# Joining the programs of attention, FFN and recurrence, and leaving out the unread matmuls

## What is computed

```
x = layernorm(x + attention(x))          # 16 heads of 16, widened to 32 latents, rotary, causal softmax
x = layernorm(x + fp4_ffn(x))            # blocks of 16 rounded to the FP4 grid before each linear layer
x = layernorm(x + recurrence(x))         # t = rmsnorm(x); 512 steps in time:
                                         #   state = tanh(state @ tanh(a) + t_step @ b)
                                         #   out   = state @ c + skip * t_step
                                         # then x + out @ w_out.T + b_out
x = layernorm(x + channel_mix(x))        # r * (relu(k)^2 @ W_v.T), each from a mix with the token before
```

## Time and profile before

| | |
|---|---|
| median of the runs shown (2317.63 and 2320.34) | 2318.99 us |
| the profiled execution: time / span | 2320.48 / 2318.7 us |
| its mean granted TensorE clock | 0.979 |
| PE busy | 2209.4 us, 95% |
| DVE busy | 1706.9 us, 74% |
| ACT busy | 1060.6 us, 46% |
| POOL busy | 1187.8 us, 51% |
| instruction packets of PE (queue q8) | 108, 1.77 MB |

### The profile page before, as it was taken

The page is one execution under the profiler, slowest core; times in us unless marked ns, Lnnn a source line. Parts: engine busy times, 40 slices in busy tenths (PEclk is TensorE's granted clock), DMA queues, the critical chain, the costliest instruction groups (busy, mean ns, idle before and its releaser), DMA issues. The chain is left out here.

```text
span 2318.7 us, 90879 instructions
## 1 busy us (share of the span) xinstructions
PE 2209.4 (95%) x36556; PEld 1542.3 (67%) x36556; DVE 1706.9 (74%) x4854; ACT 1060.6 (46%) x2707; POOL 1187.8 (51%) x1674
## 2 busy tenths in 40 slices
PE   6999999999999999959999999997999999997997
PEld 3556665556655555536777777776888888885775
DVE  3788888888887777749999999982555555454997
ACT  2656565655666665532222222231444444442444
POOL 3555555655555555525666666662444444441333
PEclk8999999999999999989999999997999999998999
DMA  2211111111111111120100000100101011011232
GB/s 92 91 56 64 57 65 65 65 63 58 57 64 65 65 61 60 52 69 22 33 32 32 32 32 32 34 20 29 32 32 36 32 34 33 32 32 46 84 95 77
DMA packets 101627, 117.73 MB, mean 51 GB/s; under 512 B 10672, under 2 KB 80080, under 8 KB 101456
## 3 DMA queue, kind: packets, MB, share of 16 engines
q1 hardware_dynamic: 101456, 115.44, 15.1%
HBM read 48.29 MB, written 33.55 MB: 35 GB/s over the span
## 5 line engine op out<-in xcount | busy, mean ns | idle before, releaser
L1474 ACT ACTIVATE r_state<-ps_state 128x64 f32<-128x64 f32 x1024 | 228.6, 223 | 295.8 <-PE ps_state L1573 290.7
L1570 PE MATMUL ps_state<-r_state,later_pairs_a 64*64 64x32 f32 x8192 | 334.4, 219 | 19.4 <-ACT r_state L1474 12.5
L1570 PEld LDWEIGHTS ps_state<-r_state,later_pairs_a 64*64 64x64 f32 x8192 | 295.2, 135 | 79.2 <-issue 60.7
L1573 PE MATMUL ps_state<-r_state,later_pairs_a 64*64 64x32 f32 x8192 | 334.6, 220 | 2.8 <-issue 2.8
L423 DVE CUSTOM_DVE_ANT_0 ps_near<-ps_near,mask 128x512 f32<-128x512 f32 (+1 forms) x512 | 270.5, 589 | 89.5 <-PE ps_near L519 89.3
L295 POOL TENSOR_SCALAR_AFFINE_SELECT probsT<-probsT 128x512 f32<-128x512 f32 x256 | 159.8, 636 | 271.2 <-ACT probsT L406 168.0
L1573 PEld LDWEIGHTS ps_state<-r_state,later_pairs_a 64*64 64x64 f32 x8192 | 288.8, 135 | 3.1 <-issue 3.1
L423 DVE CUSTOM_DVE_ANT_0 ps_far<-ps_far,mask 128x384 f32<-128x384 f32 (+1 forms) x512 | 198.3, 457 | 32.7 <-PE ps_far L519 31.7
L1158 POOL TENSOR_TENSOR f_fp<-f_rounded,f_scale 128x960 f32<-128x960 f32 (+2 forms) x67 | 117.3, 1750 | 166.2 <-DVE f_rounded L1248 166.2
L527 PE MATMUL ps_far<-Q,K 32*128 32x256 f32 (+2 forms) x1536 | 180.9, 415 | 1.2 <-ACT probsT L403 0.5
L1181 ACT ACTIVATE f_silu<-ps_gate 128x704 f32<-128x704 f32 x64 | 48.5, 758 | 288.5 <-PE ps_gate L1273 288.5
(11 more groups left out here) (213 smaller groups left out, 5401.1 us busy)
## 6 DMA issues: line engine op xcount, KB each, us to landing
q_swap<-q_sin SPq DMA_DIRECT2D x128, 128.0 KB, 2.1
k_swap<-k_sin SPq DMA_DIRECT2D x128, 128.0 KB, 2.1
xT<-in_xT_dram SPq DMA_DIRECT2D x16, 512.0 KB, 3.6
xtok<-in_x_dram SPq DMA_DIRECT2D x16, 512.0 KB, 3.8
x_rows<-x SPq DMA_DIRECT2D x16, 512.0 KB, 2.9
f_x<-x_rows SPq DMA_DIRECT2D x64, 128.0 KB, 2.0
x_rows<-f_x SPq DMA_DIRECT2D x64, 128.0 KB, 1.7
r_x<-x_rows SPq DMA_DIRECT2D x64, 128.0 KB, 2.1
```

Source lines behind the costliest of these rows:

```text
L1474: nc.scalar.activation(state[:, j % 2, banks, :, t, 0, :], sums[:, j % 2, banks, :, now], ACT.Tanh).then_inc(state_ready[t], 1)
L1570: nc.tensor.matmul(sums[half(v), j % 2, stays, c, now], A[half(v), 3 * q, c, :], last[half(v), stays, c, :], start=False, stop=True, skip_ ...
L1573: out = nc.tensor.matmul(sums[half(1 - v), j % 2, changes, c, now], A[half(v), 3 * q + 1 + was, c, :], last[half(v), changes, c, :], start ...
```

## The change

**One program per engine for three stages.** Attention, FFN and recurrence no longer open blocks. Each hands back its five programs (`Programs`), and one block runs them. The FFN's programs come as `Steps`, which can be advanced to a given step from the outside (`feed.to(n)`), so that attention issues the FFN's first steps within its last cycles, and the recurrence issues the FFN's last steps within its own beginning. Each engine does so at places of its own; for PE, attention does the FFN's first x transposes in cycle CYCLES - 1, gate and up of tile 0 in the next, tile 1 two behind that, and tile 2 behind the out projection. Only the channel mix still has a block of its own.

```diff
+class Steps:
+    def to(self, end):
+        while self.at < end:
+            if self.at == unroll and end >= self.tiles - unroll > unroll:
+                with self.engine.Fori(1, self.tiles // unroll - 1) as k:
+                    for j in range(unroll):
+                        self.step(k * unroll + j, j, k)
+                self.at = self.tiles - unroll
+            else:
+                self.step(self.at, self.at % unroll, self.at // unroll)
+                self.at += 1
...
+                if is_cycle(i, g, CYCLES):
+                    pe.wait_ge(exped, 12 * CYCLES - 2)
+                    feed.to(1)
...
+                if is_cycle(i, g, CYCLES - 1):
+                    pe.wait_ge(exped, cyc(12, i, g, 4))
+                    feed.to(0)
+                elif is_cycle(i, g, CYCLES + 1):
+                    feed.to(2)
+                elif is_cycle(i, g, CYCLES + 3):
+                    pe.wait_ge(z_added, 2 * BATCH)
+                    feed.to(3)
```

```diff
-                def fill(j, bank, times, start):
-                    for n in range(times):
-                        nc.tensor.matmul(room[:, (j + 1) % 2, bank, :], quiet[:, 0:P], quiet[:], start=start, stop=True, skip_group_check=True)
...
-                step(-1, 1)
-                with pe.Fori(0, 2) as again:
-                    with pe.Fori(again, 1 + (TILES // 2 - 1) * again) as k:
-                        for j in range(2):
-                            step(k * 2 + j, j)
-                    fill(1, TURN, 32, False)
-                step(TILES, 0)
...
+            for t in range(STEPS):
+                if first and t == LAST_FED:
+                    feed.finish()
...
+        feed.to(FED)
+        pe.wait_ge(xn_ready, 1)
+        turn(-1, 1, MIX[1])
+        feed.to(FED + 1)
+        pe.wait_ge(xT_ready, 1)
+        pe.wait_ge(*fed[0])
+        for c in range(CC):
+            out = inputs(-1, c)
...
+        step(0, 0)
+        with pe.Fori(0, TILES // 2 - 1) as k:
+            for j in (1, 2):
+                step(k * 2 + j, j % 2)
+        step(TILES - 1, 1)
+        step(TILES, 0)
```

More of the change, by code:

```diff
@@ L1 @@
+from collections import namedtuple
 from contextlib import ExitStack
@@ L42, with __init__, finish @@
 TURNED = 10 * P
+Programs = namedtuple("Programs", "sync gpsimd scalar vector tensor")
+class Steps:
+    def __init__(self, engine, step, tiles, unroll, lead, lag):
+        self.engine, self.step, self.tiles, self.unroll = engine, step, tiles, unroll
+        self.at, self.end = -lead, tiles + lag
+    def to(self, end):
+        unroll = self.unroll
+        while self.at < end:
[7 more added lines that the diff above has]
+                self.at += 1
+    def finish(self):
+        self.to(self.end)
 def head_of(g, t):
@@ L819, in attention_arrays @@
+            straight(step)
+        return Programs(sync, gpsimd, scalar, vector, tensor), early, x1_stored, (exped, 12 * CYCLES)
 def attention_arrays(inputs):
@@ L1323, with recurrence @@
 STEPS = P // BATCH
-def recurrence(nc, ident, weights, x2_dram, x3_dram):
+def recurrence(nc, sems, memory, banks, ident, weights, x2_dram, x2_stored, fed, x3_dram):
     TILES = TOKENS // P
@@ new lines, in scalar, with step @@
+    def scalar(act, feed):
+        feed.to(FED)
+        act.wait_ge(weights.loaded, 16 * weights.LOADS)
+        nc.scalar.activation(A[:], A[:], ACT.Tanh).then_inc(w_tanh, 1)
+        feed.to(FED + 1)
+        def step(i, j, k):
+            for t in range(STEPS):
+                if isinstance(i, int) and i == 0 and t == LAST_FED:
+                    feed.to(FED + 2)
+                if exists(i, 0):
+                    for q in range(SIDES):
+                        if t == 0:
+                            act.wait_ge(inputs_in, i + 1)
+                        act.wait_ge(summed[q], i * STEPS + (t + 1))
+                        if t == 0 and later(i, 0, 2):
+                            act.wait_ge(mix_full, 2 * i)
+                        now, banks = slice(t * BATCH, (t + 1) * BATCH), slice(2 * q, 2 * q + 2)
+                        nc.scalar.activation(state[:, j % 2, banks, :, t, 0, :], sums[j % 2][:, banks, :, now], ACT.Tanh).then_inc(state_ready[t], 1)
+        steps = Steps(act, step, TILES, UNROLL, LEAD, LAG)
+        steps.to(1)
+        feed.finish()
+        steps.finish()
```

2159 lines of the change are left out of this document (1112 added, 1047 removed).

## The result

The changed kernel takes 2571.74 us (median of 2 runs, 2571.54 to 2571.95) against 2318.99: 1.108 times as long, 95% interval 1.106 to 1.111. The profiled execution is one of 2571.54 us with a span of 2569.8. The forecast was 2561.

What follows compares the result with a forecast made beforehand. DVE paces the FFN, PE the recurrence; PE idles at two stage boundaries, and its clock decides. 2320.5 - 27 - 16 - 11 + 298 - 2 = 2562.5, as a median 2561 us; own range 2535 to 2585, extended down to 2262.

Steps and rivals of the forecast that it cites:

- Part 1: Attention into FFN: FFN's first steps fill PE's idle time in attention's tail; gain 27 us, bounds 20 and 31.
- Part 2: FFN into recurrence: t = 2 of tile 0 comes at 1574.3 instead of 1590.2; gain 16 us (14 to 18).
- Part 3: Recurrence loop's first pass: PE stops for new code, one stop of about 1.2 us and four of about 2.2.
- Part 4: Recurrence: a stop lowers PE's clock, nothing in the loop raises it; 62 tiles at 4.8 us more, +298 us.
- rival B: Recurrence: the clock falls and comes back after n cold tiles; 2270 + 4.8 n, with 10 tiles 2318 us; chance 0.07.
- Rival A: Recurrence: the clock holds, as no stop is placed or long enough to lower it; 2270 us, chance 0.28.

Runs made afterwards that it cites:

- a_fill16: Changed kernel with 16 unread wide bf16 matmuls (128x128, 256 columns) behind the first and last pass of the recurrence's loop: 2277.3 us, 0.982 of before.
- a_fill32: Changed kernel with the 32 unread wide bf16 matmuls back behind the first and last pass of the recurrence's loop: 2281.3 us, 0.984 of before.
- a_rows: Changed kernel with 256 unread bf16 matmuls of 128x128, 32 columns each, behind the loop's first and last pass: 2293.5 us.
- a_both: Changed kernel with 64 bf16 matmuls of 64 rows x 64, 256 columns, each twinned on the other 64 rows, behind the first and last pass: 2297.4 us.
- a_start58: Changed kernel with 58 unread matmuls right ahead of the recurrence's tile 0, none behind the first pass: 2573.9 us.
- a_fed6: Changed kernel with FFN's last step moved from t = 2 to t = 6 of the recurrence's tile 0: 2569.7 us.
- a_cols: Changed kernel with 64 bf16 matmuls of 64 rows x 64, 256 columns, between two wide ones, behind the first and last pass: 2601.2 us.

## Why the prediction was right, and where it was off

**Part 1, attention into FFN: 27 us forecast, 20.4 to 21.9 measured.** The order of work was right, the size is near the lower bound of 20. The sum assumed that PE keeps its full clock in the attention's tail, as it nearly did before. In this execution it didn't. Windows of PE from 995, after and in a_fill16, whose program is the same up to there:

```profile
995.00:1000.00 5.00, 3.26 (x22) 0.74 0.00 0
1000.00:1005.00 5.00, 4.18 (x44) 0.58 0.00 0
```

```profile
995.00:1000.00 5.00, 4.18 (x64) 1.00 0.00 0
1000.00:1005.00 5.00, 4.55 (x62) 1.00 0.01 3
```

To tell what went in the tail from what stood ahead of it, the same transposes of y at its start: before, after and a_fill16, and gate 3 of a_fill16.

```profile
993.42 0.61 PE L645 MATMUL ps_near<-squares,yT 128*128 128x128 f32 x4
```

```profile
995.37 0.61 PE L698 MATMUL ps_near<-squares,yT 128*128 128x128 f32 x4
```

```profile
992.39 0.61 PE L698 MATMUL ps_near<-squares,yT 128*128 128x128 f32 x4
...
1034.30 2.53 PE L1342 MATMUL ps_gate<-kept_w_upT,f_xT 128*128 128x352 f32 x8
```

From these transposes to gate 3 it is 68.5 us before, 44.6 after and 41.9 in a_fill16. So the join gained 26.6 us where the tail had its full clock, against 26.4 in the sum, and 23.8 in the profiled execution. The 6.6 us missing at tile 63 are then: 0.6 by which the sum was rounded up, 2.6 in the tail with its low clock (26.4 - 23.8), 2.0 by which this execution already stood behind the one of before at the tail's start (a_fill16 stood 1.0 ahead), and 1.4 that went by tile 63, at (1533.55 - 1040.00) / 60 = 8.23 us a tile in the place of 8.20. The low clock is the rule here and not the exception: of the eleven profiled executions with the merged programs nine have 0.56 to 0.75 in both windows and gate 3 at 1037.6 to 1040.0; a_fill16 and a_fill32 have 1.00 and gate 3 at 1034.3 and 1035.6. Why it falls in some and not in others is not shown.

**Part 2, FFN into recurrence: 16 forecast, 36.8 - 20.4 = 16.4 measured.** Hidden work stayed hidden.

**Part 3, stops for new code.** Forecast: about 1.2 us for the first and 2.2 for each further one at full clock, 124 matmuls apart. Measured: 1.23 and 2.22, with 123 matmul records between them and 124 up to the next stop. Then 0.97 and 1.57 at half clock. a_fill32 had 1.51, 0.48 and 2.72. From t = 2 of tile 0 to tile 2: 20.3 us, forecast 5.9 + 14 = 19.9. Of the four full-clock stops of 2.2 one happened, since the clock was gone with it.

The page "Runtime: NRT & Kernel Launch" of the Trainium skill, instruction fetch, calls the crossing of a block mostly hidden. Here it was not hidden in the loop's first pass, where four stops of 0.97 to 2.22 us came, and the lower clock behind the second. The measurement decides: hidden in the FFN, where four packets come between 1060 and 1500 for tiles of some 8.2 us, not in the recurrence, with 124 matmuls to 2.8 us.

**Part 4, the clock.** Forecast: 62 tiles of 4.8 us more, 298. Measured: 298.5 for the 61 tiles from 2 to 62. That the two agree to 0.5 us is luck. The size of a cold tile was right: 12.62 - 7.78 = 4.84 in tiles 3 to 62, sized from the seven half-clock time steps of the earlier trace rows. Tile 2 cost 7.8 more and not 4.8, with its stop of 1.57 us. The end cost less: tile 63, counted as +4.8, and -2 for the fills behind the loop against its new code make +2.8, and the measured difference from tile 63's start on is +0.3.

One sentence of the prediction was too strong: "nothing in the loop raises it". In a_fill32, a_fill16, a_rows and a_both the clock fell in tile 1, came back within 4 us on the recurrence's own matmuls, and fell again with a later stop (a_rows: 0.50 in 1564 to 1566, 1.00 in 1568 to 1570, 0.50 again from 1574). This is rival B's short cold stretch, and it did occur; B as a whole, a clock that comes back and stays, didn't. In the first passes of the other executions it didn't come back before wide matmuls ran, and in the steady loop of no kernel did it come back at all: in the changed kernel not in 60 tiles and 757 us. Why the same instructions lifted it in some first passes and not in others is open.

Together: 6.6 us from part 1, -0.4 from part 2, 0.1 from part 3, 298.5 in the place of 61 x 4.8 = 292.8 and thus 5.7, -2.5 at the end, and -0.4 since 62 x 4.8 was rounded up: 9.1 us, the gap between 2562.5 and 2571.5 of the profiled execution.

**Rival A** (clock holds, 2270 us) was priced nearly right but did not occur: a_fill16, which has the full clock from 16 wide matmuls on, measures 2277. Its condition, stops well below 2.1 us, would not have been enough: the clock went with stops of 1.51 us (a_fill32) and 1.24 us (a_start58).

## What to carry to other kernels

A pipeline that is joined better can still lose if its join held something that looked idle. Before unread matmuls are removed, find the stretch of the granted clock behind each group. Here 16 wide matmuls behind the first pass (a_fill16 has 16 more behind the last, not tested apart) turn 2571.7 us into 2277.3, and no run shows a gain from the rest of the 122. When a loop's body is long in instructions and short in time, its first pass can run at the pace of the code fetch, as here; look there for "issue" stops and for the clock behind them, and at waits for data in the same way. The fastest version of the study is the merged one with 16 wide matmuls behind the first pass: 2277.3 us, 0.982 of before (0.978 to 0.985). That is faster, but whether by 2% or more is unclear.

## What was not expected of the hardware

- PE "busy 4.00 of 4.00" says nothing about whether the clock will come back. At 0.50, a gap-free 31 us of 64-row, 32-column matmuls and 13.9 us of 64-row, 256-column ones left it there; 128 rows with 32 columns, or two times 64 rows side by side with 256 columns, brought it back in the window in which they ran.
- The same matmul of 64 rows x 64 with 256 columns has a median of 418 ns in a_cols at half clock and 269 ns in a_both, most of it at full clock.
- A clock once lost in the steady recurrence was lost for 757 us, though the stop that took it lasted 2.2.
- A stop of 1.23 us left the clock at 1.00 and one of 1.24 us in a like place did not; a wait of 1.73 us for data (a_fed6) was followed by 0.50 just as the stops for code were.
